# Query and key rows by DMA, and another order of the stages, in a two-block attention kernel

## The reference

```
x = x + block0(group_norm(x))     x = x + block1(group_norm(x))
block0: qkv = x w_qkv.T + b;  q, k, v = layer_norm(depthwise_conv3x3(.)) per head, 12 heads of 16
        attn = softmax(q k.T / 4 + rel_h[y, y'] + rel_w[x, x']),  rel_* = q . rel_pos_*[offset]
        out = (attn v + q) w_proj.T + b_proj
block1: qkv = x w + b, with a low-rank term (FacTu, q_facts / v_facts, FacTv) added to q and v
        the same attention with its own relative tables; out = (attn v) w_proj + b_proj
```

## Time and profile before

| | us |
|---|---|
| median of 3 runs | 98.87 (98.71 to 99.89) |
| the profiled execution | 98.56 |
| its span, first to last instruction | 96.4 |
| TensorE busy | 86.7 (90%) |
| VectorE busy | 55.4 (57%) |
| ScalarE busy | 50.3 (52%) |
| GpSimd busy | 30.4 (31%) |

### The profile page before, as it was taken

One profiled execution on the slowest core, in us unless ns is written; L12 is line 12 of the kernel. 1 busy time (PEld: TensorE's weight loads), 2 busy tenths in 40 slices (PEclk: granted clock), 3 DMA queues, 4 the chain that ended last, 5 costly groups with the idle time before them and its releaser, 6 DMA issues.

```text
span 96.4 us, 2468 instructions
## 1 busy us (share of the span) xinstructions
PE 86.7 (90%) x1017; PEld 60.7 (63%) x1017; DVE 55.4 (57%) x118; ACT 50.3 (52%) x119; POOL 30.4 (31%) x44
## 2 busy tenths in 40 slices
PE   5869999988999998998999997997898988979980
PEld 2138865666877887774675553993785975656450
DVE  4359998659968689657401156335795845920130
ACT  5013969666035958578844331324149368466620
POOL 7958600798999999400000000000000000000000
PEclk9999999999999999999999999999999999999999
DMA  1999700000000000000000000000000000000002
GB/s 28 315 277 292 193 0 0 0 7 0 0 0 0 14 0 0 7 0 0 7 0 0 0 0 0 0 7 0 0 0 7 0 7 0 0 7 0 0 0 82
DMA packets 2252, 3.01 MB, mean 31 GB/s; under 512 B 369, under 2 KB 1794, under 8 KB 2242
## 3 DMA queue, kind: packets, MB, share of 16 engines
q1 hardware_dynamic: 1346, 1.44, 5.7%
q10 hardware_dynamic: 752, 1.29, 4.7%
q0 software_dynamic: 144, 0.13, 0.6%
HBM read 2.66 MB, written 0.20 MB: 30 GB/s over the span
## 4 chain that ended last, share of the span: by engine, by line
PE 64%; DVE 18%; ACT 10%; DMA 3%; issue 2%
PE bank L943 9%; DVE mx L600 8%; PE bank L775 7%; PE bank L915 7%; PE bank L884 6%; PE bank L764 5%; DVE r L593 4%; PE bank L931 4%; DMA x<-x_t 3%; PE bank L862 3%; PE bank L866 3%; PE bank L788 3%; PE bank L845 2%; ACT pt L396 2%; PE bank L806 2%
## 5 line engine op out<-in xcount | busy, mean ns | idle before, releaser
L396 ACT ACTIVATE pt<-bank 128x512 f32<-128x512 f32 x24 | 13.2, 594 | 8.6 <-PE bank L915 8.5
L600 DVE TENSOR_REDUCE mx<-bank 128x2 fp32r<-128x512 f32 x24 | 15.0, 685 | 4.1 <-PE bank L884 4.0
L593 DVE TENSOR_TENSOR r<-bank,r 32x512 fp32r<-32x512 f32 x12 | 8.2, 682 | 4.4 <-ACT r L386 4.0
L749 PE MATMUL bank<-warm 128*128 128x512 bf16 x31 | 9.7, 445 | 1.0 <-POOL warm L283 1.0
L328 POOL TENSOR_SCALAR tap_p<-pad,vec 64x256 f32<-64x256 f32 (+1 forms) x11 | 10.6, 961 | 0.0
L386 ACT ACTIVATE r<-bank 32x512 fp32r<-32x512 f32 x12 | 7.0, 586 | 4.5 <-PE bank L866 4.3
L764 PE MATMUL bank<-xn,w 96*128 96x256 f32 (+1 forms) x40 | 8.2, 390 | 1.1 <-DVE xn L574 1.1
L915 PE MATMUL bank<-q,k 64*128 64x256 f32 x48 | 8.0, 315 | 1.2 <-ACT mt L392 0.9
L775 PE MATMUL bank<-pad,taps_m 128*128 128x256 f32 x36 | 8.6, 382 | 0.0
L331 POOL TENSOR_TENSOR conv_p<-conv_p,tap_p 64x256 f32<-64x256 f32 (+1 forms) x11 | 8.1, 739 | 0.9
L845 PE MATMUL bank<-hi,pick 128*128 128x256 f32 x24 | 7.5, 337 | 0.9 <-DVE lo L676 0.6
(11 more groups left out here) (109 smaller groups left out, 167.3 us busy)
## 6 DMA issues: line engine op xcount, KB each, us to landing
wp<-w_proj ACTq DMA_DIRECT2D x1, 576.0 KB, 8.2
w<-w_qkv SPq DMA_DIRECT2D x1, 432.0 KB, 8.3
w<-w_qkv SPq DMA_DIRECT2D x1, 288.0 KB, 4.9
cst<-consts ACTq DMA_DIRECT2D x1, 256.0 KB, 4.8
x<-x_t SPq DMA_DIRECT2D x1, 192.0 KB, 3.1
wpq<-w_proj_q ACTq DMA_DIRECT2D x1, 192.0 KB, 8.4
out_t<-x SPq DMA_DIRECT2D x2, 96.0 KB, 1.8
w<-w_qkv SPq DMA_DIRECT2D x1, 144.0 KB, 5.1
```

Of the source, the lines that this page charges most:

```text
L396: act.activation(pt[:, h, :, :], key_banks[h % 2][:, :].rearrange("p (k n) -> p k n", k=QT), ACT.Exp).then_inc(exped[b], 1)
L593: dve.tensor_tensor(unit_rel_dst(g, r, 1), unit_rel_src(g, r), unit_rel_dst(g, r, 0).bitcast(F32), ALU.subtract).then_inc(rel_l[b], 1)
L600: dve.tensor_reduce(mx[:, h // 4, :, 64 * (h % 2) + h % 4 // 2], ring_bank(h // 4, 4 + h % 4)[:, :].rearrange("p (q n) -> p q n", q=QT), A ...
L749: pe.matmul(to[:, :], warm[:], warm_again, start=True, stop=True)
```

## The change

- **Rows by DMA.** For group 1 of block 0 and groups 1 and 2 of block 1 the laying-out matmuls and copies are gone. SyncE issues 8 transfers for the queries and 8 for the keys of such a group, each 32 rows of 1 KB from `hi` or `lo` straight to every fourth partition of `q2` or `k2`. The partition order of `q2`, `k2`, `pick`, the relative tables and a mask column follows. The factor 1/4 moves out of the keys' selection matrices into the exponential's scale, and its inverse into GpSimd's relative windows.
- **Relative products first.** In `stage` on TensorE the relative products of group s stand ahead of the turning of group s-1's maxima, and ScalarE's order follows (high part, copied maxima, high part). The ring has six uses a group. `first_stage` is written out apart.
- **Third tile first.** In block 0, D is centred and normalised ahead of C. C's convolution is spread over later places, its variance, turning to tokens and the first weighing stand in `stage(0, 2)`.
- **Free banks.** The last group's second key pair has banks 4 and 0 to itself, `variance` of C and E have the other half of their tile's bank, so that `cen_e` is not needed, the second low-rank product has bank 5 and stands between the blocks.

The core of the diff:

```diff
-        ring = [bank[6], bank[0], bank[1], bank[4]]
-        key_banks = bank[2:4]
+        ring = [bank[1], bank[4], bank[6], bank[0]]
+        key_banks = [bank[2], bank[3], bank[2], bank[3]] * 2 + [bank[2], bank[3], bank[4], bank[0]]
+        pick_banks = {(0, 0): (bank[6], bank[0]), (0, 2): (bank[5], bank[5]), (1, 0): (bank[6], bank[0])}
...
-        cen_order = [A, B, C, D, E]
+        cen_order = [A, B, D, C, E]
...
+        by_dma = ((0, 1), (1, 1), (1, 2))
...
+            def q_by_dma(b, g):
+
+                sp.wait_ge(lo_set[b], 3 if g == 2 else 1)
+                for j in range(2):
+                    t, i = q_place(4 * g + 2 * j)
+                    for k, part in enumerate((hi, hi, lo, lo)):
+                        sp.dma_start(q2[k:128:4, 2 * g + j, :].bitcast(F32),
+                                     part[16 * i:16 * i + 32, place3[t], :].bitcast(F32)).then_inc(q_rows[b, g], 16)
+
+            def k_by_dma(b, g):
+
+                sp.wait_ge(lo_set[b], 3 if g == 2 else 2)
...
+            for b, g in by_dma:
+                q_by_dma(b, g)
+                k_by_dma(b, g)
...
-                    pool.tensor_copy(rel_w[:, k, :, first:first + 16], src).then_inc(rel_set, 1)
+                    pool.tensor_scalar(rel_w[:, k, :, first:first + 16], src, HD ** 0.5, None, ALU.mult).then_inc(rel_set, 1)
...
                 g = s - 1
                 rel_high(b, s, 0)
+                copy_maxima(b, g)
                 rel_high(b, s, 1)
...
+            stage(0, 1, {0: lambda: tile_rstd(D), 1: d_and_c, 2: lambda: move_q(0, 2)})
+            stage(0, 2, {0: lambda: tile_rstd(C), 3: lambda: tile_stats(E)})
             last_stage(0)
...
+            stage(0, 0, {0: lambda: taps(D, 3, D_SPLIT)})
+            add_lora(0)
+            stage(0, 1, {0: lambda: normalise(D), 1: lambda: low(D)})
+            move_k(0, 2)
+            stage(0, 2, {0: lambda: normalise(C), 1: v_to_tokens})
             normalise(E)
...
                 if t == D:
-                    pe.wait_ge(logged, n_cen[C])
-                if t == E:
-                    pe.wait_ge(e_copied, 1)
+                    pe.wait_ge(w1_set, 1)
...
-                if h >= 1:
+                if h >= 1 and (g, j) != (HG - 1, 1):
                     pe.wait_ge(exped[b], h)
...
+            def first_stage(b, between={}):
+
+                pick_unit(b, 0, 0)
                 if 0 in between:
                     between[0]()
+                rel_units(b, 0)
+                pick_unit(b, 0, 1)
                 if 1 in between:
                     between[1]()
+                score_pair(b, 0, 0)
+                score_pair(b, 0, 1)
                 if 2 in between:
                     between[2]()
+
+            def stage(b, s, between={}):
+
+                g = s - 1
+                rel_units(b, s)
+                if 0 in between:
+                    between[0]()
+                turn_maxima(b, g)
+                if 1 in between:
+                    between[1]()
+                pair_by_key(b, g, 0)
+                if 2 in between:
+                    between[2]()
+                score_pair(b, s, 0)
+                score_pair(b, s, 1)
+                if 3 in between:
+                    between[3]()
+                pair_by_key(b, g, 1)
+                if 4 in between:
+                    between[4]()
+                if g >= 1:
+                    spread_sums(b, g - 1)
                 if 5 in between:
                     between[5]()
...
+            def c_first():
+                convolve(C, 1, 2, 4)
                 lora_second(0)
 
+            first_stage(0, {0: lambda: convolve(C, 1, 0, 2), 1: c_first, 2: lambda: centre_tile(D)})
+            stage(0, 1, {0: lambda: variance(D), 1: lambda: convolve(C, 1, 4, 6), 3: lambda: convolve(C, 1, 6, TAPS), 4: lambda: pick_unit(0, 2, 0), 5: lambda: pick_unit(0, 2, 1)})
+            stage(0, 2, {1: lambda: variance(C), 2: lambda: turn(C), 3: lambda: weigh(0, 0), 5: lambda: centre_tile(E)})
             last_stage(0)
...
+            first_stage(1, {0: lambda: project_v(1), 1: project_rest, 2: lambda: warm_up(3, bank[2])})
+            stage(1, 1, {1: lambda: add_input(1, 0)})
+            stage(1, 2, {1: lambda: weigh(1, 0)})
             last_stage(1)
```

More of the change, by code:

```diff
@@ L250, in unit_rel_dst, with n_moved @@
             return r2[64 * r + 32 * low:64 * r + 32 * low + 32, 2 * g:2 * g + 2, :]
-        def late_k(b, s):
-            return b == 0 and s == 0
+        by_dma = ((0, 1), (1, 1), (1, 2))
+        def n_moved(b, g):
+            return sum((b, k) not in by_dma for k in range(g + 1))
         def ring_bank(g, n):
-            return ring[n % 4]
+            return ring[(6 * g + n) % 4]
         def unit_rel_src(g, r):
-            return ring_bank(g, 2 + r)[0:32, :].rearrange("p (n j) -> p j n", j=2)
-        lora_ps = bank[5][0:HALF, 0:2 * DIM].rearrange("p (t n) -> p t n", t=2)
+            return ring_bank(g, r)[0:32, :].rearrange("p (n j) -> p j n", j=2)
+        lora_ps = [bank[i][0:HALF, 0:2 * DIM].rearrange("p (t n) -> p t n", t=2) for i in (3, 5)]
         block = ctx.enter_context(nc.Block())
@@ L531, in _ @@
             high1(B)
-            stage(1, 0)
+            first_stage(1)
             high1(D)
@@ L683, in _ @@
             low(A)
-            taps(D, 0, 2)
+            taps(D, 0, 3)
             def k_in():
@@ L727, in _ @@
             low1(B)
-            stage(1, 0)
-            low1(D)
-            stage(1, 1, {1: v_in})
+            stage(1, 0, {0: lambda: low1(D)})
+            v_in()
+            stage(1, 1)
             stage(1, 2)
@@ L858, in rel_units @@
                 heads = [q2[rows, 2 * g:2 * g + 2, :].rearrange("p j (y x) -> p y x j", x=SIDE) for rows in PARITY]
-                out = [ring_bank(g, 2 + r)[:, :].rearrange("p (y x j) -> p y x j", j=2, x=SIDE) for r in range(2)]
+                out = [ring_bank(g, r)[:, :].rearrange("p (y x j) -> p y x j", j=2, x=SIDE) for r in range(2)]
                 for y in range(SIDE):
@@ L883, in score_pair @@
                         for r, rows in enumerate(PARITY):
-                            mm = pe.matmul(ring_bank(g, 4 + 2 * j + r)[:, q * TOK:(q + 1) * TOK], (q2, r2)[part][rows, pair, cols],
+                            mm = pe.matmul(ring_bank(g, 2 + 2 * j + r)[:, q * TOK:(q + 1) * TOK], (q2, r2)[part][rows, pair, cols],
                                            hot2[rows, :] if part else k2[rows, pair, :], start=(part == 0), stop=(part == 1))
@@ L922, in weigh @@
                 pe.wait_ge(v_set[b], 1 if b == 0 and g < HG - 1 else 2)
-                if b == 0 and g == 0:
-                    pe.wait_ge(w1_set, 2)
                 if b == 1 and g == 0:
@@ L1106, in _ @@
             group_sums(1)
-            warm_up(5, bank[2])
+            lora_second(1)
+            warm_up(3, bank[2])
             project(1, 0, A, w1)
```

228 lines of the change are left out of this document (96 added, 132 removed).

## The result

The changed kernel takes 109.45 us (median of 4 runs, 108.49 to 110.84); before takes 98.79 beside it. The ratio is 1.105, interval 1.098 to 1.113: slower by 10.5%, outside the range of 94.8 to 100.0. Ratios are taken to runs of before made beside each kernel, and these lie at 98.2 to 99.0 or at 99.5 to 100.3 us, so medians of different kernels compare to about 1 us only. The start up to the first maximum takes 25.1 to 27.0 us in the profiles of the changed kernel's family, and 28.9 in one, though most of their edits lie behind it. So the experiments are read by the stretches behind that event first, and by the total second.

What follows compares the result with a forecast made beforehand. TensorE was taken to bound the first block, a chain across engines the second. Second block -3.9 and first block +2.3 gave -1.6 us from 98.87, so 97.3 us; range 94.8 to 100.0.

Steps and rivals of the forecast that it cites:

- the spacing of SyncE's issues: Second block's 32 transfers on SyncE's queue: start to start 0.42 us, bounds 0.37 and 0.49, last landing 1.1 us early.
- The times at which the forecast wants the rows: Second block: last rows of the four transfer series wanted at 68.9, 72.4, 74.5 and 77.9.
- slower, by the queue: Rival: last key rows land late and hold the second block's group 2 scores; 99.7 to 101.8 us; chance 0.17.
- The second block's chain: Second block: relative products ahead of the turning make score to score 5.55 for 6.97; direct sums 3.9 us earlier.
- The first stage's gain of 0.47: Second block: key layout behind relative products, key copy on ScalarE; scores at 66.85 in place of 67.32.
- its last stage: Second block: weighing ahead of the first key pair, second pair in its own banks; worth 0.6 us.
- The first block's holes: First block: TensorE idle 1.5 us before C's turning to tokens and 1.4 before group 0's weighing; block 2.3 later.
- a rival of 0.05 and 3 us: Clock falls in the first block's holes, later matmuls run at 1.2 GHz: 3 us more, 100.3; chance 0.05.
- Two rivals: Late transfer queue in the second block, chance 0.17, and clock falling in the first block's holes, chance 0.05.
- First block keeps its lead: Rival: first block's holes close, its loss of 2.3 shrinks to nothing, 95.0 us; chance 0.27, wholly or mostly.

Runs made afterwards that it cites:

- the runs that mend this: Changed kernel with the second block's 16 key transfers on GpSimd's queue: 100.64 us alone, 97.68 us with the third tile's turning and group 0's weighing also moved.
- the run with two queues: Changed kernel with the second block's 16 key transfers issued by GpSimd, the 16 query transfers left on SyncE: 100.64 us (1.011).
- the combined run: Changed kernel with both edits: second block's keys on GpSimd's queue, third tile's turning and group 0's weighing moved behind group 2's scores: 97.68 us (0.989).
- The undone order: Kernel with keys on GpSimd and turning and weighing moved, but the turning of maxima again ahead of the relative products: 99.34 us (1.009).
- the run with filling: Changed kernel with seven warm-up matmuls ahead of the third tile's turning and six ahead of group 0's weighing: 106.6 us (1.074).

## Why the prediction was wrong

**The term that failed is the spacing of SyncE's issues.** I took 0.42, with bounds 0.37 and 0.49, because 32 rows lie between one row and 128. It is 0.64, for 32 rows and for 128, plus now and then a pause of 0.5 to 1 us. The times at which the forecast wants the rows held within some 0.4 us in the runs that mend this (group 2's scores 16.3 behind the first issue, forecast 15.9), and with 0.64 its own sum has the last keys at 62.0 + 31 x 0.64 + 1.8 = 83.6, 5.7 us after they are wanted; with the pauses it is 7.5 in the profile after (93.1 on its clock, from 69.75 + 21.3 + 2.1, wanted 15.9 behind the first low part). That is the rival "slower, by the queue", to which I gave 0.17, and which I priced at 0.6. With pauses it came out at 7.8 (39.3 for the 31.5 of the run with two queues), some 0.8 of it by the clock that fell while TensorE waited. It was not only the last keys that were late: the last query row, wanted at 74.5, came 5.6 late as well. The bounds were the fault: loads from main memory at the kernel's start were no row for a transfer within on-chip memory, and I said that no row showed the shape but kept the bound of 0.49 for the range.

**The second block's chain was right in its sum, and by some luck.** Forecast: 5.55 from score to score, gain 3.9. With rows in time: 5.7 in the combined run, and a block of 31.1 to 31.5, so 3.3 to 3.8 less than before's 34.85. The first stage's gain of 0.47 was 0.37 to 0.39 (8.50 from the normalised input to the first maximum, for 8.87). The undone order shows that the gain of a stage comes where I said. But up to group 2's scores the combined run has gained 2.8 of my 3.3 us, and its last stage 1.0 where I had 0.6: two misses that cancel.

**The first block's holes were right, their price was not.** I had 1.5 us of idle ahead of the third tile's turning: 1.50. I had 1.4 ahead of the weighing: 0.94 for what is left of it at half clock. I had the block 2.3 us longer, and it is 5.6 longer from first maximum to its end, with 0.4 planned ahead of that. The clock took 2.2 or more, which I had as a rival of 0.05 and 3 us. Without it 3.4 remain, and with the 0.4 ahead 3.8 for my 2.3. By the run with filling nearly all of the 1.5 that are missing stand in two places: from group 1's maxima to group 2's it takes 10.7 for my 10.1, and from there to the block's end 17.2 for the 16.4 that my terms give, the latter with filling that can overrun a hole. In the combined run it is 3.0 more than before behind group 2's maxima, for some 1.5 by my terms without the hole. So the work that the change puts there was priced too low as well. Moving the turning and the weighing gives 3.8 back at once, so their place makes both holes and the fall of the clock; the 1.8 that stay are the order's other price.

**Two rivals came true together.** I had priced each alone, as if one excluded the other, and left 0.12 beyond 100.85. But nothing excludes both: they act in different blocks, and the late rows let the clock fall a second time. The sum of the span's 12.2 us: +4.5 in the second block, +5.6 +0.4 in the first, and 1.7 of a slow start in this one profile. "First block keeps its lead" is refuted by the 1.50 alone.

**The Trainium skill's rule** (DMA: Bandwidth & Descriptors, Rules for kernel authors), that small transfers pay mostly overhead, holds in its direction. But the overhead that decided is not the fixed 2.0 us of a transfer, which its section Anatomy of one DMA gives for transfers that GpSimd issues, and which these rows show on both queues (1.9 to 2.1 on SyncE, 2.1 on GpSimd): it is the issuing queue's 0.59. The same page (Issuing engines are not separate DMA queues) says that issuing from several engines only saves the sequencer's issue time, usually small beside the transfer; here it is 0.59 beside some 2 us, but 32 of them stand in a row, and moving 16 made the second block 7.8 us shorter.

## What to carry to other kernels

Many small transfers are paid at the queue that issues them: multiply their number by the spacing of that kind of transfer, compare the landing of the last with the time at which it is wanted, and split them over idle queues before giving the idea up. If no row shows a transfer of that kind, leave the upper bound open. And an operation whose input comes late belongs behind the work that could run in the meantime: besides its own wait it can cost the clock of what follows, here for some 7 us. And a product that runs beside other work in one order can stand in the way in the next, as the laying-out products did: price what is removed in the new order and not in the old.

## What the runs showed of the hardware

- An issue on SyncE's queue took 0.59 to 0.60 us (medians) for a transfer from on-chip memory to on-chip memory, of 32 or 128 rows, contiguous or to every fourth partition; the first of a series was 0.47 to 0.62. From main memory three of six took 0.42 us, the others 0.60, 0.87 and 1.34. ScalarE's own took 0.52 to 0.79 within on-chip memory, GpSimd's 0.53. In long runs of issues on SyncE single ones take 1.1 to 1.8 us (5 of 48 in the profile after). What that pause is was not tried.
- TensorE's granted clock fell to 0.50 in a stretch in which TensorE had waited 1.50 us and was busy for 0.50 of 2.00 us, and came back some 7 us later; in the first block of the run with both edits, where no wait is longer than 0.78 us, it stayed at 1.00.
